# Row maxima from high halves in two row groups, and remainders made two tiles at a time, in a masked attention

## What is computed

```python
# 16 heads of 32 columns; q is the layer's own x, k and v are the context; mask is [4, 1, 1024, 1024]
scores = jnp.einsum('bhqd,bhkd->bhqk', qh, kh) * scale
scores = jnp.where(mask == 0, jnp.float32(-1000000000.0), scores)
probs = jax.nn.softmax(scores, axis=-1)
atten = jnp.einsum('bhqk,bhkd->bhqd', probs, vh)
```

## Time and profile before

| | us |
|---|---|
| median of 3 runs | 3126.95 (3123.92 to 3128.47) |
| the profiled execution: its time | 3123.28 |
| the profiled execution: its span | 3121.1 |
| cross phase, first row maximum to last value matmul | 1162.6 to 2101.4 |
| POOL's remainders of the cross phase | 1189.1 to 2100.6 |

### The profile page before, as it was taken

How to read it: one execution, slowest core, us unless ns; L and a number is a source line. 1 busy time by engine, 2 the same in 40 slices (tenths; PEclk the granted TensorE clock), 3 DMA queues, 4 the chain that set the end, 5 groups by cost and what they waited for, 6 DMA issues and landing times. The chain is left out here.

```text
span 3121.1 us, 77095 instructions
## 1 busy us (share of the span) xinstructions
PE 2634.2 (84%) x24119; PEld 1431.1 (46%) x24119; DVE 2318.2 (74%) x4525; ACT 1762.4 (56%) x3255; POOL 1874.1 (60%) x1424
## 2 busy tenths in 40 slices
PE   7999478888886869999999999980999899703999
PEld 3555235555554534555555555550444344301444
DVE  8888667777775767888888888867333467697776
ACT  3444257777775435666666666654233477696333
POOL 3444479999997317999999999996100144300000
PEclk9999779999998988999999999995999999856999
DMA  8999724444445662222122131115644588797332
GB/s 305 336 334 342 267 96 134 136 126 131 135 133 169 235 202 60 53 75 66 51 80 62 49 98 50 47 54 172 214 153 158 200 278 281 258 415 282 110 126 81
DMA packets 320920, 511.28 MB, mean 164 GB/s; under 512 B 35669, under 2 KB 155221, under 8 KB 320810
## 3 DMA queue, kind: packets, MB, share of 16 engines
q1 hardware_dynamic: 317674, 503.65, 48.3%
q0 software_dynamic: 1952, 6.29, 0.6%
q10 hardware_dynamic: 1184, 0.01, 0.0%
HBM read 270.95 MB, written 194.28 MB: 149 GB/s over the span
## 5 line engine op out<-in xcount | busy, mean ns | idle before, releaser
L1102 POOL TENSOR_TENSOR cross_plo<-cross_p 128x1024 f16<-128x1024 f32 x448 | 906.6, 2058 | 73.4 <-ACT cross_p L940 69.7
L940 ACT ACTIVATE cross_p<-cross_st 128x512 f32<-128x512 f32 x1024 | 556.2, 595 | 289.1 <-PE cross_st L874 289.0
L1015 DVE CUSTOM_DVE_ANT_0 cross_junk<-cross_sc,rows 128x1024 bf16<-128x1024 f32 x512 | 619.0, 1219 | 110.5 <-PE cross_sc L835 98.2
L1102 POOL TENSOR_TENSOR self_plo<-self_p 128x1024 f16<-128x1024 f32 (+7 forms) x512 | 577.0, 1165 | 19.1 <-ACT self_p L940 18.8
L940 ACT ACTIVATE self_p<-self_st,self_strip 128x512 f32<-128x512 f32 (+3 forms) x768 | 415.3, 582 | 148.0 <-PE self_st L872 116.8
L1015 DVE CUSTOM_DVE_ANT_0 self_junk<-self_sc,self_strip 128x1024 bf16<-128x1024 f32 (+7 forms) x512 | 371.1, 752 | 140.8 <-PE self_sc L835 136.0
L869 PE MATMUL cross_st<-cross_qa,cross_ka 97*128 97x512 f16 x1024 | 390.4, 381 | 2.5 <-ACT cross_p L940 1.7
L874 PE MATMUL cross_st<-rows,idbig 128*128 128x512 f16 x1024 | 389.9, 381 | 0.0
L835 PE MATMUL cross_sc<-cross_ka,cross_qa 96*128 96x512 f16 x1024 | 311.3, 386 | 22.3 <-DMA cross_ka<-scr_k_hi 16.7
L897 PEld LDWEIGHTS cross_o<-cross_vh,cross_p 128*128 128x128 bf16 x4096 | 270.1, 97 | 75.0 <-issue 21.7
L897 PE MATMUL cross_o<-cross_vh,cross_p 128*128 128x65 f16 x4096 | 297.4, 191 | 4.6 <-POOL cross_plo L1102 4.2
(11 more groups left out here) (254 smaller groups left out, 5710.3 us busy)
## 6 DMA issues: line engine op xcount, KB each, us to landing
self_strip<-self_strips SPq DMA_DIRECT2D x68, 516.0 KB, 3.2
scr_gate<-gt_y SPq DMA_DIRECT2D x96, 256.0 KB, 2.1
v_w<-scr_gate SPq DMA_DIRECT2D x96, 256.0 KB, 4.1
scr_h<-v_w SPq DMA_DIRECT2D x96, 256.0 KB, 4.0
j_h<-scr_h SPq DMA_DIRECT2D x48, 512.0 KB, 9.6
d_o<-scr_o SPq DMA_DIRECT2D x9, 1536.0 KB
scr_up<-v_y SPq DMA_DIRECT2D x48, 256.0 KB, 4.3
j_u<-scr_up SPq DMA_DIRECT2D x24, 512.0 KB, 12.0
```

The source lines that it names most:

```text
L940: nc.scalar.activation(p32[u % NPR][:, q0:q1], stp[cc % 2][:, 0:q1 - q0], ACT.Exp, bias=bias, scale=SM).then_inc(expd, 1)
L1015: nc.vector.tensor_tensor_reduce(junk[slot % 2][:, 0:w], sc[slot % 2][:, 0:w], bias, 1.0, -3e38, ALU.add, ALU.max, qmax[n % 2][:, qt:qt + ...
L1102: nc.gpsimd.tensor_tensor(plo[u % NPR][:, q], p32[u % NPR][:, q], high[:, q], ALU.subtract).then_inc(lo_g, 1)
```

## The change

It changes the cross phase in two places.

First, the scores for the row maxima: instead of two matmuls over 96 rows (three products of halves), one matmul takes the high halves of the first 512 keys over rows 0 to 31, and a second those of the last 512 keys over rows 32 to 63. For the second, a new tile `kx` holds the high halves of keys 512 to 1023 in its rows 32 to 63; one more DMA a head loads it, so `qk_in` counts 112 a head (`QKS`). Rows 32 to 63 of `qa` already hold q_hi. The products with low halves are left out of the maxima alone; the key scores keep them.

Second, the tiles of p: `p32` and `plo` become four tiles of twice the width (`NPP`, `PW`), each for two neighbouring units (`spot`). In the cross phase POOL makes the remainders of both units in one instruction, after the second unit's exponentials; unit 5, whose neighbour DVE makes, is done alone (`lows_of`). In the causal phase each unit still has an instruction of its own, and its columns now begin at the start of its half.

```diff
+        SLEAD, ELEAD, NPP = 19, 6, 4
+        NPR = PAIR * NPP
+        PW = PAIR * S
+        kx = [sb(f"kx{j}", [2 * HD, GT], F16) for j in range(0 if causal else NQK)]
-        p32 = [sb(f"p32_{j}", [P, S], F32) for j in range(NPR)]
-        plo = [sb(f"plo{j}", [P, S], F16) for j in range(NPR)]
+        p32 = [sb(f"p32_{j}", [P, PW], F32) for j in range(NPP)]
+        plo = [sb(f"plo{j}", [P, PW], F16) for j in range(NPP)]
...
+        QKS = 96 if causal else 112
...
+        def spot(u):
+
+            return u // PAIR % NPP, 0 if u % PAIR == 0 else S
...
+        def lows_of(u):
+
+            j, b = spot(u)
+            if on_vector(u) or not causal and u % PAIR == 0 and not on_vector(u + 1):
+                return None
+            if not causal and u % PAIR == 1 and not on_vector(u - 1):
+                return j, 0, b + width(u)
+            return j, b, b + width(u)
...
+                    if not causal:
+                        sp.dma_start(kx[j][HD:2 * HD, :], k_dram[0].rearrange("b r t -> (b r) t")[ds(row, HD), GT:S]).then_inc(qk_in[j], 16)
...
+                    if not causal:
+                        nc.tensor.matmul(sc[slot % 2][:, 0:GT], qa[j][0:HD, qt * P:(qt + 1) * P], ka[j][0:HD, 0:GT], start=True, stop=True)
+                        nc.tensor.matmul(sc[slot % 2][:, GT:S], qa[j][HD:2 * HD, qt * P:(qt + 1) * P], kx[j][HD:2 * HD, :],
+                                         start=True, stop=True).then_inc(scored, 1)
+                        return
...
                 def low(i, u):
-                    n, at, kt = keys_of(u)
-                    if on_vector(u):
+                    if lows_of(u) is None:
                         return
                     pool.wait_ge(expd, i * CS + chunks_by(u) + 2)
-                    q = slice(*query_range(n, kt))
-                    high = p32[u % NPR][:].bitcast(BF16).rearrange("p (q h) -> p q h", h=2)[:, :, 1]
-                    nc.gpsimd.tensor_tensor(plo[u % NPR][:, q], p32[u % NPR][:, q], high[:, q], ALU.subtract).then_inc(lo_g, 1)
+                    j, a, z = lows_of(u)
+                    high = p32[j][:, a:z].bitcast(BF16).rearrange("p (q h) -> p q h", h=2)[:, :, 1]
+                    nc.gpsimd.tensor_tensor(plo[j][:, a:z], p32[j][:, a:z], high, ALU.subtract).then_inc(lo_g, 1)
```

More of the change, by code:

```diff
@@ L532, in _ @@
                                                         u65[:, :, v * TG + n, 0:HD], ALU.subtract).then_inc(ul_done, 1)
-SLEAD = 19
-ELEAD = 6
 NQK = 4
-NPR = 8
 UH = ST
@@ L547 @@
 PRIME = 3 * UH
+PAIR = 2
 def attention_phase(nc, c, name, causal, q_dram, k_dram, v_dram, out_dram, mb_dram=None, nm_dram=None, place_dram=None, kept=None, spare=None):
@@ L677, in on_vector, with width, high_of, lows_by @@
             return not causal and u % UH == 4
-        def lows_before(u, vector):
-            return sum(on_vector(m) == vector for m in range(u))
-        LV, LG = lows_before(HB * UH, True), lows_before(HB * UH, False)
+        def width(u):
+            n, k, kt = keys_of(u)
+            a, z = query_range(n, kt)
+            return z - a
+        def spot(u):
+            return u // PAIR % NPP, 0 if u % PAIR == 0 else S
+        def high_of(u):
+            j, b = spot(u)
+            return p32[j][:, b:b + width(u)].bitcast(BF16).rearrange("p (q h) -> p q h", h=2)[:, :, 1]
+        def lows_of(u):
+            j, b = spot(u)
+            if on_vector(u) or not causal and u % PAIR == 0 and not on_vector(u + 1):
[3 more added lines that the diff above has]
+            return j, b, b + width(u)
+        def lows_by(u, vector):
+            if vector:
+                return sum(on_vector(m) for m in range(u + 1))
+            return sum(lows_of(m) is not None for m in range(u + 1)) + (lows_of(u) is None)
+        LV, LG = lows_by(HB * UH - 1, True), sum(lows_of(m) is not None for m in range(HB * UH))
         def within(last, u):
@@ L815, in _ @@
                 for j in range(NQK):
-                    sp.wait_ge(qk_in[j], 96 * (NI + 1))
+                    sp.wait_ge(qk_in[j], QKS * (NI + 1))
                     sp.wait_ge(v_in[j], 16 * (NI + 1 if j < NQK - 1 else NI))
@@ L829, in scores @@
                     if at == 0:
-                        pe.wait_ge(qk_in[j], (i + n // NQK + 1) * 96)
+                        pe.wait_ge(qk_in[j], (i + n // NQK + 1) * QKS)
                     pe.wait_ge(taken, i * (HB * UH) + slot + 1)
+                    if not causal:
[3 more added lines that the diff above has]
+                        return
                     k0, k1 = key_range(n, qt)
@@ L885, in values @@
                     if on_vector(u):
-                        pe.wait_ge(lo_v, i * LV + lows_before(u, True) + 1)
+                        pe.wait_ge(lo_v, i * LV + lows_by(u, True))
                     else:
-                        pe.wait_ge(lo_g, i * LG + lows_before(u, False) + 1)
+                        pe.wait_ge(lo_g, i * LG + lows_by(u, False))
                     a, z = query_range(n, kt)
-                    high = p32[u % NPR][:].bitcast(BF16).rearrange("p (q h) -> p q h", h=2)[:, :, 1]
+                    j, b = spot(u)
+                    high, rest = high_of(u), plo[j][:, b:b + width(u)]
                     for qt in range(a // P, z // P):
-                        q = slice(qt * P, (qt + 1) * P)
+                        q = slice(qt * P - a, qt * P - a + P)
                         out = ob[qt // 4]
@@ L897, in values @@
                         nc.tensor.matmul(out[:, qt % 4, :], high[:, q], vh[n % NQK][:, kt, :], start=first, stop=False, skip_group_check=True)
-                        mm = nc.tensor.matmul(out[:, qt % 4, 0:HD + 1], plo[u % NPR][:, q], vh[n % NQK][:, kt, 0:HD + 1],
+                        mm = nc.tensor.matmul(out[:, qt % 4, 0:HD + 1], rest[:, q], vh[n % NQK][:, kt, 0:HD + 1],
                                               start=False, stop=last_kt, skip_group_check=True)
@@ L939, in exps @@
                         bias = strip[n % NQK][:, S + kt:S + kt + 1] if causal else 0.0
-                        nc.scalar.activation(p32[u % NPR][:, q0:q1], stp[cc % 2][:, 0:q1 - q0], ACT.Exp,
+                        nc.scalar.activation(p32[j][:, b + q0 - a:b + q1 - a], stp[cc % 2][:, 0:q1 - q0], ACT.Exp,
                                              bias=bias, scale=SM).then_inc(expd, 1)
@@ L1026, in low @@
                     dve.wait_ge(expd, i * CS + chunks_by(u) + 2)
-                    q = slice(*query_range(n, kt))
-                    high = p32[u % NPR][:].bitcast(BF16).rearrange("p (q h) -> p q h", h=2)[:, :, 1]
-                    nc.vector.tensor_tensor(plo[u % NPR][:, q], p32[u % NPR][:, q], high[:, q], ALU.subtract).then_inc(lo_v, 1)
+                    j, b = spot(u)
+                    q = slice(b, b + width(u))
+                    nc.vector.tensor_tensor(plo[j][:, q], p32[j][:, q], high_of(u), ALU.subtract).then_inc(lo_v, 1)
                 def gather(i, n):
```

## The result

The changed kernel is slower: 3176.27 us (3174.31 to 3177.75, 4 runs) against 3127.71 us for the kernel before, run beside it. The ratio is 1.0148, with a 95% interval of 1.0127 to 1.0168. That is 48.6 us more where 29 less were forecast.

The account below looks back on a forecast made before the run. PE was taken to set the pace, POOL 0.11 us a head behind; after the change POOL would be last at 13.73. Terms -29.6 + 0.4 + 0.5 = -29 from 3126.95 gave 3098 us; eight in ten 3086 to 3150.

Parts of the forecast that it names:

- What bounds the kernel: Cross phase before: PE sets the pace at 14.28 us a head, with POOL 0.11 us behind.
- The price of POOL's pair: Cross-phase remainders: one POOL instruction for two units costs 3.56 us instead of 3.70, saving 0.43 a head.
- The stretching: Lengthening of POOL's remainders put down to DVE's remainder and output scaling: 1.19 us a head, assumed unchanged.
- The switch: PE going between whole array and row groups, 16 times a head, each taken to cost 0.03 to 0.05 us.
- the turn: Once-a-head PE place with 8 columns of weights, nearest row to a shape change: next matmul 0.11 us later, nothing paid.
- full tail of 0.165: Matmul record of 0.381 us beyond its place of 0.216; if a switch drains it all, PE wants 15.42 a head.
- the point at which I had said that it decides: PE's step from scores to key scores and back: from 0.094 us a switch on, it decides.
- the stretching left at 1.19: POOL's cross-phase sum: DVE's lengthening of its remainders stays 1.19 us a head, so POOL wants 13.73.
- two score banks carry the longer pieces: DVE's maxima in the cross phase: 1.15 to 1.2 us each against 1.72 a unit, so longer instructions cause no delay.
- A stretching that grows with its length: Sign of a wrong forecast: the lengthening of POOL's remainder instructions rises as they get longer; no size given.
- The third rival: Draining the array at PE's row-group changes decides: slower, 3197 us at 0.165 each, 3291 at 0.26; nearly all of 26%.

Follow-up runs that it names:

- Pairs alone with the scaling on ACT: Changed kernel with maxima scores over 96 rows as before, POOL's remainders in pairs, output scaling moved from DVE to ACT: 3128.71 us, ratio 1.0006.
- Rows alone: Changed kernel, but POOL makes each unit's remainder by itself again; scores stay in row groups: 3117.42 us, ratio 0.9977.
- the scaling on ACT: Full changed kernel with the masked attention's output scaling moved from DVE to ACT, as eight products in four steps: 3117.86 us, ratio 0.9981.
- two units in a row: Full changed kernel, output scaling on ACT, PE making the maxima's scores of two units one behind the other every second step: 3082.46 us, ratio 0.9874.

## Why the prediction was wrong

- **What bounds the kernel** was read rightly: PE first, POOL 0.11 us behind. Pairs alone with the scaling on ACT leave the time at 1.0006: taking work off POOL wins nothing while PE is as before. The numbers are a little high, since the two rows of maxima of the earlier trace rows are 14.28 us apart and the mean period of a head is 14.24.
- **The price of POOL's pair** held: 3.60 us for a record, less 0.04 of overlap, against 3.56. The stretching fell from 1.19 to about 0.95 us a head, which was not foreseen.
- **The switch** was mis-sized. I took 0.03 to 0.05 by the nearest row, the turn. Measured are 0.11 - 0.03 on the way in and 0.32 - 0.22 on the way out, so about 0.09 each: the point at which I had said that it decides. The turn's 8 columns of weights were no change of the kind in question. The Trainium skill's rule (TensorEngine Tiling (Array Packing), Key Properties), that a change of tiling mode drains the array, agrees with these distances in kind; no full tail of 0.165 is paid. With this term right PE wants 12.78 + 16 x 0.09 = 14.22 us a head, 0.06 under before, which over 61.6 heads is about 3123: still no loss. Rows alone and the scaling on ACT have this term without DVE's long wait and ran 3117 and 3118, with 14.12 and 14.11 us a head; the sum is a little too high, since the two score matmuls start within 0.01 us of each other and not 0.028 apart. So POOL would not have been last, as the forecast has it, and of the 78 us between 3098 and 3176 this term is some 23 (29 less than before were forecast, 6 less were measured with the scaling on ACT).
- **The step that failed**, and turned the forecast's sign, is "With the stretching left at 1.19 (DVE's two instructions are still there once a head)", with its companion "two score banks carry the longer pieces". I read the contention between POOL and DVE from POOL's side alone, as a lengthening of POOL's records that the diff would not touch. It has another side: DVE waits for the end of POOL's instruction, and that wait grows with the instruction's length. Its price, 0.65 us becoming 2.36 once a head, took DVE from the forecast's 12.35 us a head to about 13.6 (0.90 of 15.10), and went through the two score tiles to PE (a hole of 1.1 us a head) and by the missing exponentials to POOL (1.58). It is some 55 of the 78 us: against before, the kernel with the scaling on ACT is 6 us faster and the one with it on DVE 49 us slower.
- The sign was in the trace of before: the scaling's median of 652 ns against its minimum of 424, by which it already waited for POOL. I looked at the first and not at the second. "A stretching that grows with its length", which I named as a sign against me, came, but on DVE.
- **The third rival** had the right sign, a chance of 26% and the wrong mechanism: the switch alone (rows alone, 0.9977) makes the kernel no slower. None named a wait of DVE.

## What to carry to other kernels

When two engines share something, ask for each of them what the other's longest instruction does to it: merging instructions on one saves its fixed cost, here 0.14 us each, and makes the other wait up to the whole length. Compare an instruction's median with its minimum in the trace before you merge. A switch into row groups and back cost here 0.18 us, about as much as the two small matmuls brought, so put as many row-group matmuls behind one another as buffers allow. The scaling on ACT turned the loss of 1.5% into a gain of 0.2%, and two units in a row on top of it made that 1.3%.

## What the runs showed of the hardware

- Instructions of DVE with two SBUF inputs and POOL's remainders wait for each other's end, in both directions: POOL's 3.60 became 4.31 behind DVE's remainder, DVE's 0.42 became 2.36 and 3.50 behind POOL's pair. DVE's row maxima, with one input in PSUM, ran beside POOL at 1.21 to 1.23 us all the while. The Trainium skill has the rule, and I had not drawn on it (SBUF — State Buffer, SBUF: two separate sides): whichever of the two starts first holds the shared ports for the whole instruction, and the other is blocked. The numbers above agree with it.
- A wait of 0.93 us once a head left PE's granted clock at 1.00 (2.4 GHz). Behind one of 2.66 it was 0.50 (1.2 GHz) for two units of the head shown, which cost another 2.6 us.
- The way into row groups took 0.11 us from the last value matmul, with one group in use or two; the way out 0.31 to 0.32 from the start of the last score matmul, where 0.215 is usual.
